# A graph layer's edge sort: when the counts are made, how the slots are decoded, which engine makes the moments, which queue carries what

## What is computed

```python
h = relu(layernorm(x))
x = x + segment_sum(relu(concat([h[src], h[dst]], 1) @ W0.T + b0), src, 1250)
h = relu(layernorm(x))
out = segment_sum((h @ W1.T)[src] * edge_weight[:, None], dst, 1250)
x = x + where(out >= 0, out, alpha * out)
```

## Time and profile before

| | us |
|---|---|
| median of the runs | 1008.88 |
| lowest, highest of 3 | 1006.73, 1010.54 |
| the profiled execution | 1017.97 |
| its span, first to last instruction | 1016.2 |
| the sort, to the first step behind its last product | 271.9 |
| mean granted clock of TensorE | 0.975 |

### The profile page before, as it was taken

The page is one execution under the profiler, slowest core; times in us unless marked ns, Lnnn a source line. Parts: engine busy times, 40 slices in busy tenths (PEclk is TensorE's granted clock), DMA queues, the critical chain, the costliest instruction groups (busy, mean ns, idle before and its releaser), DMA issues.

```text
span 1016.2 us, 20178 instructions
## 1 busy us (share of the span) xinstructions
PE 972.9 (96%) x4719; PEld 781.0 (77%) x4720; DVE 872.2 (86%) x1747; ACT 775.0 (76%) x1650; POOL 643.0 (63%) x934
## 2 busy tenths in 40 slices
PE   5799999999799999999999999999999999999998
PEld 5477778787678887788878778878888788778776
DVE  6989988897769999999999999999999888873444
ACT  4887878778788888888888888888888776755210
POOL 2478877767477777777777777777777755530000
PEclk9689999899989999999999999999999999999999
DMA  8000000000021111111111111111111100010011
GB/s 220 4 3 4 2 4 2 4 2 3 19 62 42 44 42 41 40 42 43 41 43 42 40 40 41 43 42 41 44 41 42 31 30 30 24 42 1 21 41 40
DMA packets 35923, 35.16 MB, mean 35 GB/s; under 512 B 7778, under 2 KB 32095, under 8 KB 35876
## 3 DMA queue, kind: packets, MB, share of 16 engines
q1 hardware_dynamic: 31176, 33.95, 10.7%
q0 software_dynamic: 4416, 0.30, 1.7%
q10 hardware_dynamic: 284, 0.33, 0.1%
HBM read 30.92 MB, written 3.29 MB: 34 GB/s over the span
## 4 chain that ended last, share of the span: by engine, by line
PE 68%; DVE 2%; ACT 1%; issue 1%; POOL 0%; POOLq 0%
PE node_ps L1166 8%; PE edge_ps L1205 8%; PE edge_ps L1211 8%; PE edge_ps L1210 8%; PE edge_ps L1206 8%; PE node_ps L1167 8%; PE m_ps L1177 4%; PE psum L1309 3%; PE psum L1311 3%; PE psum L1310 3%; PE m_ps L1291 1%; PE edge_ps L1269 1%; PE edge_ps L1270 1%; PE edge_ps L1261 1%; PE edge_ps L1266 1%; PE edge_ps L1265 1%
## 5 line engine op out<-in xcount | busy, mean ns | idle before, releaser
L1398 ACT ACTIVATE msg_hi<-edge_ps 128x512 fp32r<-128x512 f32 x332 | 197.6, 595 | 60.8 <-PE edge_ps L1211 60.7
L1122 POOL TENSOR_TENSOR M<-M,pair_w 125x125 f32 x332 | 160.7, 484 | 126.9 <-DVE pair_w L1545 97.2
L1559 DVE SCALAR_TENSOR_TENSOR msg_lo<-edge_ps,msg_hi 128x512 fp32r<-128x512 f32 x332 | 223.6, 683 | 17.3 <-ACT msg_hi L1398 13.0
L417 POOL DMA_INDIRECT edge_table<-fields,row_no x136 | 170.4, 1253 | 58.2 <-issue 47.4
L844 ACT ACTIVATE lane_piece<-hot_lane,fields 125x128 fp32r<-125x128 bf16 x498 | 153.8, 392 | 12.1 <-DVE hot_lane L504 11.8
L705 PE MATMUL psum<-hot_tile,lane_piece 125*128 125x384 f32 x582 | 145.8, 373 | 9.2 <-ACT lane_piece L844 6.3
L1106 POOL TENSOR_TENSOR hot_w<-hot_d,weight_l 128x252 fp32r<-128x252 bf16 x166 | 140.0, 843 | 0.0
L1166 PE MATMUL node_ps<-msg_hi,hot_s 128*125 128x512 f32 x332 | 135.1, 407 | 0.0
L1205 PE MATMUL edge_ps<-b_hi,turned_d 125*128 x332 | 132.7, 400 | 0.7 <-ACT turned_d L1382 0.7
L1211 PE MATMUL edge_ps<-a_lo,turned_s 125*128 x332 | 131.9, 397 | 0.0
L1210 PE MATMUL edge_ps<-a_hi,turned_s 125*128 x332 | 131.4, 396 | 0.2 <-ACT turned_s L1382 0.2
(11 more groups left out here) (258 smaller groups left out, 2044.8 us busy)
## 6 DMA issues: line engine op xcount, KB each, us to landing
spread<-edge_rows SPq DMA_DIRECT2D x190, 125.0 KB
out_dram<-result SPq DMA_DIRECT2D x10, 224.0 KB
edge_table<-fields,row_no POOLq DMA_INDIRECT x136
w_in<-in_L_gnn_W_dram SPq DMA_DIRECT2D x1, 2048.0 KB, 12.7
S<-in_x_dram SPq DMA_DIRECT2D x1, 1792.0 KB
w_in<-in_L_gnn_W_dram SPq DMA_DIRECT2D x1, 1024.0 KB, 5.1
S<-in_x_dram SPq DMA_DIRECT2D x1, 448.0 KB
edge_table<-zeros SPq DMA_DIRECT2D x1, 384.0 KB, 14.9
```

The lines of the kernel that those rows point to most:

```text
L417: pool.indirect_dma_start(table_dram[:, :], bass.IndirectOffsetOnAxis(ap=row_no[:, c:c + 1], axis=0), fields[:, c, 0:TABLE_FIELDS], None). ...
L1122: pool.tensor_tensor(part, part, pair_w[h][:, j, 0, 0:BN], ALU.add).then_inc(m_added, 1)
L1398: act.activation(msg_hi[j][:], edge_ps[j][:], ACT.Relu).then_inc(hi_ready, 1)
L1559: dve.scalar_tensor_tensor(out=msg_lo[j][:], in0=edge_ps[j][:], scalar=0.0, in1=msg_hi[j][:].bitcast(F32), op0=ALU.max, op1=ALU.subtract). ...
```

## The change

All edits are in the sort. In words:

- *Counts*: all five chunks are counted before the loop: 0 and 1 where they were, 2 to 4 behind the prefixes of chunk 0; ScalarE copies them there. `bases` runs three times, for chunk 0, chunk 1 and chunks 2 to 4 together (behind columns 1 and 12 of chunk 0), over one long `running` row.
- *Slots*: `slots(k, step)` has ten steps; chunk 0's follow each other, those of later chunks stand two behind a column, from column 30 to 34. The prefixes start behind column 8. For k > 0 the first pick is a multiplication, so the memset goes.
- *W0*: parts 2 and 3 are turned before the prefixes of chunk 0, and a piece (`weights_part`) follows each of the first 14 prefixes: two subtractions, then for each later pair four half turns and two subtractions.
- *Moments*: VectorE makes them by block (`moment`: stats, aggregate, reciprocal, shift), block 0 before the loop, block b inside it, 16 columns ahead; ScalarE makes one square root a block (`deviation`) and one at its very start.
- *Transfers*: W0 goes to ScalarE's queue, the zeros to GpSimd's; the larger part of x is issued behind the first base row; base_lo and base_up of chunk 0 go to ScalarE's queue.
- *Code word*: GpSimd puts it together in nine operations. The bias rows for the product are padded to 128 partitions.

```diff
-BASES_AT, PREFIX_AT, PICK_AT, SLOTS_AT = 4, 9, 14, 30
-COUNT_BACK, COPY_BACK = 7, 3
+BASES_AT, PREFIX_AT, PICK_AT, SLOTS_AT = (1, 12), 8, 14, 30
+BASE_PARTS = ((0, CHUNK), (CHUNK, 2 * CHUNK), (2 * CHUNK, ECOLS))
+SLOT_STEPS, STEPS_A_COLUMN = 10, 2
 STEP = 16
+MOMENTS_AT, STD_AT = (2, 3, 11, 12), 4
...
+COUNT_BANKS = ((4, 5), (0, 2), (0, 2), (6, 7), (4, 5))
 def count_ps(k):
-    return [psum[0:NBLK, bank, 0:HALF * NBLK] for bank in ((0, 2) if k == 1 else (4, 5))]
+    return [psum[0:NBLK, bank, 0:HALF * NBLK] for bank in COUNT_BANKS[k]]
...
-for part, blocks in enumerate(X_PARTS):
+def load_x(part):
     for rows in SPLIT:
-        sp.dma_start(S[rows, blocks], x.rearrange("(b p) d -> p b d", p=BN)[rows, blocks]).then_inc(x_in[part], 16)
-    if part == 0:
-        sp.dma_start(w_in[:], w0.rearrange("(o p) i -> p o i", p=P)).then_inc(w_loaded, 16)
+        sp.dma_start(S[rows, X_PARTS[part]],
+                     x.rearrange("(b p) d -> p b d", p=BN)[rows, X_PARTS[part]]).then_inc(x_in[part], 16)
+load_x(0)
 sp.dma_start(bias_row[:], b0.rearrange("(a d) -> a d", a=1)).then_inc(small_in, 16)
 sp.dma_start(alpha_t[:], alpha.rearrange("(a d) -> a d", a=1).to_broadcast([P, 1])).then_inc(small_in, 16)
-sp.wait_ge(cleared, 1)
-sp.dma_start(table_dram[1:1 + P * NT].rearrange("(p t) f -> p (t f)", p=P),
-             zeros.rearrange("p t f -> p (t f)")).then_inc(cleared_dram, 16)
 def counts_by_bucket(k):
     sp.wait_ge(count_out, k + 1)
-    if k > 0:
-        sp.wait_ge(scan_step, k)
-    sp.dma_start(counts[:, 2:CHUNK + 2], counts_out[:]).then_inc(counts_in, 16)
+    sp.dma_start(counts[:, k * CHUNK:(k + 1) * CHUNK], counts_out[:, k]).then_inc(counts_in[min(k, 2)], 16)
+def rows_of_bases(k):
+    for r, part in enumerate((base_hi, base_lo)):
+        sp.wait_ge(base_rows, 2 * min(k, 2) + r + 1)
+        if k > 0 and r == 0:
+            sp.wait_ge(picked, k * NPICK)
+        sp.dma_start(hot[EROWS + r:EROWS + r + 1], part[:, k * CHUNK:(k + 1) * CHUNK]).then_inc(rows_in, 16)
 counts_by_bucket(0)
-for k in range(NCHUNK):
-    for r, part in enumerate((base_hi, base_lo)):
-        sp.wait_ge(base_rows, 2 * k + r + 1)
-        sp.dma_start(hot[EROWS + r:EROWS + r + 1], part[:]).then_inc(rows_in, 16)
-    if k == 0:
-        sp.wait_ge(upper_row, 1)
-        sp.dma_start(hot[EROWS + 2:EROWS + 3], base_up[:]).then_inc(upper_in, 16)
-    if k + 1 < NCHUNK:
-        counts_by_bucket(k + 1)
+counts_by_bucket(1)
+sp.wait_ge(base_rows, 1)
+sp.dma_start(hot[EROWS:EROWS + 1], base_hi[:, 0:CHUNK]).then_inc(rows_in, 16)
+load_x(1)
+rows_of_bases(1)
+for k in range(2, NCHUNK):
+    counts_by_bucket(k)
+for k in range(2, NCHUNK):
+    rows_of_bases(k)
...
+pool.wait_ge(cleared, 1)
+pool.dma_start(table_dram[1:1 + P * NT].rearrange("(p t) f -> p (t f)", p=P),
+               zeros.rearrange("p t f -> p (t f)")).then_inc(cleared_dram, 16)
...
+pool.wait_ge(pairs_ready, 1)
+pair_of, part, upper_bits = blk_a[:, 1, :], local[:, 1, :], local[:, 0, :]
+own(pool.tensor_scalar(part, node_f[:, 0, :], float(TILE), None, ALU.mult))
+own(pool.tensor_tensor(upper_bits, part, node_f[:, 1, :], ALU.add))
+own(pool.tensor_scalar(part, blk[:, 0, :], -float(BN * TILE), None, ALU.mult))
+own(pool.tensor_tensor(upper_bits, part, upper_bits, ALU.add))
+own(pool.tensor_scalar(part, blk[:, 1, :], -(UPPER / 2 + BN), None, ALU.mult))
+own(pool.tensor_tensor(upper_bits, part, upper_bits, ALU.add))
+own(pool.tensor_scalar(part, pair_of, UPPER, float(SHIFT_S * TILE + 1) - UPPER, ALU.mult, ALU.add))
+own(pool.tensor_tensor(upper_bits, part, upper_bits, ALU.add))
+pool.tensor_scalar(fields[:].bitcast(I32)[:, :, CODE_AT], upper_bits, 65536.0, None,
+                   ALU.mult).then_inc(code_ready, 1)
...
+def bases(part):
+    first, last = BASE_PARTS[part]
+    cols = slice(first, last)
+    dve.wait_ge(counts_in[part], 16 * (last - first) // CHUNK)
+    dve.tensor_tensor_scan(running[:, first + 1:last + 1], keep[:, cols], counts[:, cols],
+                           running[:, first:first + 1], ALU.mult, ALU.add).then_inc(scan_step, 1)
+    dve.wait_ge(scan_step, part + 1)
+    dve.tensor_copy(base_hi[:, cols], running[:, cols]).then_inc(base_rows, 1)
+    dve.wait_ge(base_rows, 2 * part + 1)
+    dve.tensor_tensor(base_lo[:, cols], running[:, cols], base_hi[:, cols],
+                      ALU.subtract).then_inc(base_rows, 1)
...
+if k > 0 and g == 0:
+    dve.tensor_tensor(planes[:, 0:nb, :].rearrange("p b c -> p (b c)"), psum[0:EROWS, 3 + n % 3, 0:nb * CHUNK],
+                      hot[0:EROWS, 0:nb, :].rearrange("p b c -> p (b c)"), ALU.mult).then_inc(picked, 1)
+    return
...
+if step == 0:
+    dve.wait_ge(picked, (k + 1) * NPICK)
+    used = planes[:, 0:2 * PICK if k == 0 else PICK, :]
+    mark(dve.tensor_reduce(slot[:], used.rearrange("p b c -> p c b"), AX.X, ALU.add))
+    return
+dve.wait_ge(vstep, steps[0])
+if step == 1:
...
+if step == 6:
+    mark(dve.tensor_tensor(after, whole, upper, ALU.subtract))
+    mark(dve.scalar_tensor_tensor(out=at, in0=whole, scalar=-float(TILE), in1=slot[:], op0=ALU.mult, op1=ALU.add))
...
+def moment(b, stage):
+    if stage == 0:
+        dve.wait_ge(x_in[0 if b < X_PARTS[0].stop else 1], 32)
+        dve.bn_stats(stats[:, b, :], S[0:BN, b, :]).then_inc(moments, 1)
+        return
+    dve.wait_ge(moments, 4 * b + stage)
+    if stage == 1:
+        dve.bn_aggr(mv[:, b, :], stats[:, b, :]).then_inc(moments, 1)
+    if stage == 2:
+        dve.wait_ge(std_ready, b + 1)
+        dve.reciprocal(rstd[0:BN, b:b + 1], std[:, b:b + 1]).then_inc(moments, 1)
+    if stage == 3:
+        dve.scalar_tensor_tensor(out=shift[0:BN, b:b + 1], in0=mv[:, b, 0:1], scalar=-1.0,
+                                 in1=rstd[0:BN, b:b + 1], op0=ALU.mult, op1=ALU.mult).then_inc(moments, 1)
...
+    if s < 8:
+        moment(0, s - 6)
 for g in range(NPICK):
     pick(0, g)
-slots(0)
+    if g in (8, 10):
+        moment(0, g // 2 - 2)
+for step in range(SLOT_STEPS):
+    slots(0, step)
...
+b, stage = divmod(q + STEP, STEP)
+if 0 < b < NBLK and stage in MOMENTS_AT:
+    moment(b, MOMENTS_AT.index(stage))
 b, stage = divmod(q - REST_AT, STEP)
 if stage == 0 and 0 <= b < NBLK:
     low_of_h(b)
 if k + 1 < NCHUNK:
     if i < NBLK:
         hot_of_block(k + 1, i)
-    if i == NBLK:
-        dve.memset(planes[:, 0:PICK, :], 0.0).then_inc(planes_clear, 1)
-    if i == BASES_AT:
-        bases(k + 1)
+    if k == 0 and i in BASES_AT:
+        bases(BASES_AT.index(i) + 1)
     for g in range(NPICK):
         if i == PICK_AT + g:
             pick(k + 1, g)
-    if i == SLOTS_AT:
-        slots(k + 1)
+    for step in range(SLOT_STEPS):
+        if i == SLOTS_AT + step // STEPS_A_COLUMN:
+            slots(k + 1, step)
+    if i == FIRST[k + 1] - FIRST[k] - 1:
...
+pe.wait_ge(hot_made, k * NBLK + -(-(g * PICK + nb) // NBLK))
...
+def weights_part(n):
+    if n < 2:
+        low_w(2 + n)
+        return
+    pair, part = divmod(n - 2, 6)
+    i = 2 * (pair + 2) + part // 2 % 2
+    if part < 4:
+        turn_w(i, range(part % 2 * 2, part % 2 * 2 + 2))
+    else:
+        low_w(2 * (pair + 2) + part - 4)
...
+count(0)
 pe.wait_ge(spread_done, 1)
 pe.matmul(total_ps, ones[0:HCOLS * NBLK, 0:EROWS], spread_sum.rearrange("p s d -> p (s d)"),
           start=True, stop=True).then_inc(totals, 1)
-count(1, range(CHUNK))
+count(1)
 pe.wait_ge(w_loaded, 16)
 pe.wait_ge(act_own, 2)
-weights(0)
+turn_w(0, range(KC))
+turn_w(1, range(KC))
+low_w(0)
+low_w(1)
+turn_w(2, range(KC))
+turn_w(3, range(KC))
 pe.wait_ge(slot_bases, 1)
 pe.matmul(base_col_ps, tile_base[0:1, :], ones[0:1, 0:1], start=True, stop=True).then_inc(base_col, 1)
-weights(1)
 for g in range(NPICK):
     prefix(0, g)
-weights(2)
-weights(3)
+    if g < 14:
+        weights_part(g)
+pe.wait_ge(count_out, 2)
+count(2)
+pe.wait_ge(w_lo, 2 * KC)
+count(3)
+pe.wait_ge(picked, NPICK)
+count(4)
 pe.wait_ge(base_out, 1)
-pe.wait_ge(count_out, 2)
+pe.wait_ge(count_out, NCHUNK)
...
-part = i - last + COUNT_BACK
-if k + 2 < NCHUNK and 0 <= part < 3:
-    count(k + 2, range(CHUNK // 3 * part, CHUNK // 3 * (part + 1)))
...
+act.dma_start(w_in[:], w0.rearrange("(o p) i -> p o i", p=P)).then_inc(w_loaded, 16)
+act.wait_ge(dconst, 1)
+act.activation(std[:, 0:1], eps_t[0:BN, :], ACT.Sqrt)
...
+def deviation(b):
+    act.wait_ge(moments, 4 * b + 2)
+    act.activation(std[:, b:b + 1], mv[:, b, 1:2], ACT.Sqrt, bias=eps_t[0:BN, :]).then_inc(std_ready, 1)
...
+copy_counts(1)
 turned_weights(0)
-act.wait_ge(mix_bases, 2)
-act.activation(base_up[:], bases_at[:, 1:2].to_broadcast([NBKT, CHUNK]), ACT.Copy,
+act.wait_ge(mix_bases, 1)
+act.activation(base_up[:], mix_at[:].to_broadcast([NBKT, CHUNK]), ACT.Copy,
                bias=-float(MID_TILE) * UPPER, scale=UPPER).then_inc(upper_row, 1)
+act.wait_ge(upper_row, 1)
+act.dma_start(hot[EROWS + 2:EROWS + 3], base_up[:]).then_inc(upper_in, 16)
+act.wait_ge(base_rows, 2)
+act.dma_start(hot[EROWS + 1:EROWS + 2], base_lo[:, 0:CHUNK]).then_inc(rows_in, 16)
 turned_weights(1)
```

(17 more changed lines are left out.)

## The result

The changed kernel takes 1014.61 us (median; 1012.78 to 1016.03) and the kernel before, on the same chip, 1010.38 (1006.73 to 1012.43): the ratio is 1.0051, with a 95% interval of 1.0037 to 1.0065. It is slower by half a per cent. The forecast was 1003.3 us in a range of 998 to 1012: the time lies outside of it, and the sign is wrong. The profiled execution of the changed kernel took 1013.81 us.

What follows compares the result with a forecast made beforehand. No single engine was taken to bound the kernel; the sort's gain goes straight to the end. First column +4.4, chunk 0 +1.7, middle three -9.1, tail -2.6 sum to -5.6 on median 1008.9: 1003.3 us, range 998 to 1012.

Steps and rivals of the forecast that it cites:

- first column: Start of the sort: VectorE's first column comes at 47.2 us, 4.4 later than before; ends 44.9 and 51.7.
- chunk 0: Sort's first chunk, first column to end of decoding chunk 1: 45.6 us instead of 43.9, +1.7.
- middle three: Stretches between the decodings of chunks 1 to 4: 44.0 us each, 132.0 against 141.1, -9.1; ends 43.3 and 46.
- tail: From the last decoding to the sort's end: the scatter table becomes the last arrival, 41.6 us instead of 44.2, -2.6.
- the quiet base_up row: Before the first prefix: a small row landing 2.7 us after issue (26.99 to 29.70), taken as the counts' landing time.
- Rival (b): Contention with GpSimd operations and x's 2 MB eats the start: first column at 50, chunks 44.5, 1007.6 us; chance 0.18.
- First product: Chunk 0's first product, after counting three chunks, a copy and three pieces of W0: near 50.5 us, against 52.8 before.
- GpSimd's scatters hold a chunk at 43.3: Middle chunks: 28 scatters of 1.548 us take 43.3 us, which sets how far a chunk can shrink.
- In none is an engine full: Sort of the kernel before: no engine fills a stretch; VectorE works 40.1 to 41.9 us of the middle three.
- Rival (a): Longer prologue, no faster loop: first column at 49.5, chunks stay at 47.0 us, 1014.7 us in all; chance 0.13.
- rival (d): Loop: spreading the decoding does nothing, so 1.0 us a chunk is not won, 1007.3 us; chance 0.10.
- rival (c): Scatters become the sort's only limit: first column at 45.0, sort ends at 260.6, 997.6 us; chance 0.13.

Runs made afterwards that it cites:

- second before: The kernel before, run and profiled once more with no edit: 1010.15 us, span 1008.4.
- the fastest kernel: The changed kernel with x's larger part held back, 132 scatters instead of 136 and the code word on VectorE: 999.52 us, ratio 0.9894 to the kernel before.

## Why the prediction was wrong

Its own cut of the sort, beside what the two executions and the kernel after show (us; "first column" counts from the start of the span):

| part | profiled before | forecast | after | second before |
|---|---|---|---|---|
| first column | 42.7 | 47.2 | 50.6 | 41.4 |
| chunk 0 | 43.9 | 45.6 | 42.0 | 41.4 |
| middle three | 141.1 | 132.0 | 124.2 | 137.9 |
| tail | 44.2 | 41.6 | 52.0 | 44.3 |
| end of the sort | 271.9 | 266.3 | 268.8 | 265.0 |

The forecast was 11.3 us too low. 6.9 of it is the profiled execution: its sort was that much longer than in the second one, and the 5.6 us that the forecast won were counted from there. 1.5 is the median of before, 1008.9 of three runs and 1010.4 of ten. 3.4 is the first column, less 1.0 that the rest was shorter than forecast (218.2 instead of 219.2); 0.5 remains. That makes 6.9 + 1.5 + 3.4 - 1.0 + 0.5 = 11.3.

**The baseline.** The text saw that the execution stood 9.1 us above the median and moved the median "by the same amount". This step fails: an execution that is slow has its excess somewhere, here 6.9 us in the sort itself, and the change was credited with removing part of it. 3.2 of it lie in the middle three, whose stalls the change was to end, 1.3 before the first column and 2.5 in chunk 0. Had the sum gone to 266.3 from 265.0, the forecast would have been 1.3 us slower, within the bound of no change.

**Start to the first pick.** The wait for the counts went, as forecast. The first prefix was put at 29.0 and came at 34.3. The failed step is "the counts could land like the quiet base_up row, 2.7 us after its issue" and its silent extension to base_lo: the sum took the lower bound, 2.7, for a row that travels beside x, when the upper bound of 8.6 came from just such a case, 13 KB beside large loads. 8.1 us were measured, and 2.6 with x held back. Up to there the text was right: its row was to leave at 24.9 + 1.5 = 26.4 and left at 26.15, so the whole miss of 5.3 us is in how long it travelled. Rival (b) had named it. The Trainium skill (DMA: Bandwidth & Descriptors, "Issuing engines are not separate DMA queues") says that transfers started by different engines share the same 16 DMA engines and interleave; the trace agrees, and moving base_lo to ScalarE's queue did not take it out of x's way. GpSimd's operations (the nine, then the copies of the weights) delay the scan by 3.2 us (24.07 instead of 20.90), between the bounds of 0 and 7.4. 1.5 was taken for what would show behind ScalarE's lateness; the row leaves 1.7 later for it (26.15 instead of 24.44), which gives about 2 at the end once x is away, and next to nothing before. Of the 9.2 us that the start lost against the second execution of before, 7.1 go with x held back and 1.6 more with the code word on VectorE; the rest is 0.5 to 1.0.

**Picks, W0 and decoding of chunk 0.** Forecast 13.7 us for the prefixes with their pieces of W0, measured 46.11 - 34.26 = 11.9; decoding 4.5, and 4.5 measured. The mechanism was right and the pieces were cheaper. The kernel with W0's work behind the picks shows that the interleaving costs at most 1.5 us at the first column and earns it back.

**First product.** Forecast 50.5, measured 52.8, behind a first column that is 3.4 later. Right in kind.

**Chunk 0 and the middle three.** Forecast 45.6 and 3 x 44.0, measured 42.0 and 41.4 on average. The failed step is "GpSimd's scatters hold a chunk at 43.3". They don't hold it: nothing in a column waits for a scatter. VectorE runs on at its own 41 us, and GpSimd falls behind by the difference. Forecast and measurement nearly agree on VectorE's balance without stalls (41.9 forecast, 40.3 to 41.9 busy). "In none is an engine full" passes over TensorE, which in the earlier trace rows is busy for 43.6 to 47.3 us of the three stretches of 45.7 to 48.6 and had VectorE wait for it; after the change it is 40.1 to 40.4, and those waits are gone. Rival (a), no faster loop, fell, and that its 1014.7 us is the measured time within 0.1 is chance: its loop was to stay at 47.0 a chunk and its tail to shrink. The doubled counting shows that the counting was on the path, and the decoding in one piece that rival (d), that spreading does nothing, fell too: 1.3 us a chunk, where 1.0 was forecast.

**The tail.** Forecast 41.6, measured 52.0. "The table last" was right; its size was not, because the lag of the scatters arrives there. 112 scatters of the first four chunks take the chain from 51.5 to 51.5 + 112 x 1.568 = 227.1, 10.3 us behind the decoding at 216.8. Then come 24 more (37.6) and 4.1 to VectorE's start: 10.3 + 37.6 + 4.1 = 52.0. Of the 13.7 us that the loop won over the second execution of before, the tail gives back 7.7 and chunk 0 0.6; 5.4 remain, less than the 9.2 that the start lost. That VectorE's wait of 13.58 us is so near to 13.7 is no sum: it stood 2.78 us at the same place before.

**The sum was right by cancelling.** From the first column 219.2 were forecast and 218.2 measured, with its terms off by -3.6, -7.8 and +10.4 us. The 218.2 themselves are no chance, since the chain of scatters gives the sum whatever the columns do: 0.9 to the first, 135 x 1.568 = 211.7, and 5.6 behind the last make 218.2. This is rival (c), which the text priced at 210.5 + 4.2 and gave a start at 45.9. So what happened is (c)'s limit with (b)'s start, a pair that none of the rivals stood for: (c) was counted as the fast case because its start was assumed early.

**The range.** Its upper bound was to run "to the upper ends of start and chunks". By the text's own terms these are 51.7 and 46 us, and 1008.9 + 8.9 + 1.7 - 3.1 - 2.6 = 1013.8, so 1012 was drawn 2 us too low. The ends of the start don't add up either: 27.5 + 13.4 + 4.5 is 45.4, not 44.9, and 27.5 + 3.9 + 16.3 + 4.5 is 52.2, not 51.7.

**The signs to look for.** Right: no wait for counts, prefixes and turning alternating (for 11.9 us, not 13 to 16), no low clock from 180 to 190, the table after the last product, nothing behind the sort changed. Wrong: the first column (50.6), the first product (52.8), 44 us between decodings, and GpSimd's wait of 1 us a chunk, which was none. The last was the best sign of all: it says which chain ends last. None of the three signs by which the text would have called itself wrong came: the chunks fell to 41 and 42, the first column stayed short of 51, and nothing behind the sort changed. They watched the terms, and the fault was in which chain the terms were of.

## What to carry to other kernels

Where two chains run side by side and meet only at the end, write each one's end as start plus count times duration and take the later; shortening the other below it buys nothing, and whatever delays the first link of the longer one costs its full length. Look at a second execution before stalls of the first are counted as a gain, above all when it stands away from the median. Hold a large load back until the small row on which everything waits has landed: one wait on SyncE's queue was worth 7.2 us here. With four scatters less and the code word back on VectorE besides, the change became 1.1% faster than the kernel before instead of 0.5% slower.

## What the runs showed of the hardware

- A 13 KB transfer on ScalarE's queue beside 2 MB just issued on SyncE's reached its reader 8.1, 8.9 and 9.5 us after its issue (the kernel after, with fewer scatters, with the code word on VectorE); with the 2 MB held back it took 2.5 to 2.6 us in five kernels. Another queue gave it no precedence.
- Small VectorE steps beside GpSimd operations on 330 columns: 0.82 instead of 0.21 us (subtraction), 0.80 instead of 0.35 (scan), 0.98 instead of 0.23 (subtraction with a narrower output). GpSimd's work beside it made the chain to the scan 3.2 us longer.
- A chain of indirect transfers issued by GpSimd took 1.54 to 1.58 us for each over 200 us, waits for row numbers left out (1.548 and 1.561 in the two executions of before, 1.568 after, 1.582 in the fastest kernel).
- The sort of the same program took 271.9 us in one execution and 265.0 in another, with granted clocks of 0.84 and 0.92 in chunk 0, 0.96 and 1.00 in the third stretch, 0.93 and 0.96 in the fourth. Whether the clock makes the difference, or what else starts it, no run here settles.
